# A signed gate maximum in place of absolute gate values, and a new split of gate tiles between two stages

## The reference, cut to what matters

```python
def act_qdq(x):
    qmax = 2.0 ** (ACT_BITS - 1) - 1.0
    scale = jnp.maximum(jnp.max(jnp.abs(x)) / qmax, 1e-12)
    return jnp.clip(jnp.round(x / scale), -qmax - 1.0, qmax) * scale
x = act_qdq(x)
up = act_qdq(x @ lpbq_dequant(w_up).T)
gate = act_qdq(x @ lpbq_dequant(w_gate).T)
sig = fixed_qdq_u16(jax.nn.sigmoid(gate))
gate = act_qdq(gate * sig)
o = act_qdq(gate * up)
return o @ lpbq_dequant(w_down).T
```

## Time and profile before

| | us |
|---|---|
| median of three executions | 1949.89 |
| lowest and highest of them | 1949.58 and 2811.03 |
| the profiled execution, timed from outside | 1950.04 |
| its span, first to last instruction | 1948.1 |
| TensorE busy in the span | 1710.1 (88%) |
| VectorE busy | 1481.2 (76%) |
| ScalarE busy | 1187.5 (61%) |
| GpSimd busy | 809.7 (42%) |

### The profile page before, as it was taken

One profiled execution on the slowest core, in us unless ns is written; L12 is line 12 of the kernel. 1 busy time (PEld: TensorE's weight loads), 2 busy tenths in 40 slices (PEclk: granted clock), 3 DMA queues, 4 the chain that ended last, 5 costly groups with the idle time before them and its releaser, 6 DMA issues. The chain is left out here.

```text
span 1948.1 us, 25419 instructions
## 1 busy us (share of the span) xinstructions
PE 1710.1 (88%) x9112; PEld 659.3 (34%) x9112; DVE 1481.2 (76%) x2113; ACT 1187.5 (61%) x1911; POOL 809.7 (42%) x442
## 2 busy tenths in 40 slices
PE   0899999999999999999968999999999910299999
PEld 0222333323333333333214454544444400044444
DVE  5899888888888888888745665548999998855452
ACT  2376677767777777776642232229997678854441
POOL 3388888978889888886610010100000000000000
PEclk9999999999999999999988999999999965599999
DMA  5477786756776766766344556648785357755542
GB/s 152 92 191 191 164 192 161 160 133 142 183 175 152 164 152 142 169 158 139 69 129 162 185 190 206 183 143 268 254 268 192 120 180 258 237 179 177 168 163 76
DMA packets 188157, 332.17 MB, mean 171 GB/s; under 512 B 27488, under 2 KB 106720, under 8 KB 179520
## 3 DMA queue, kind: packets, MB, share of 16 engines
q1 hardware_dynamic: 179104, 265.54, 44.2%
q0 software_dynamic: 8928, 65.02, 16.7%
HBM read 171.90 MB, written 93.45 MB: 136 GB/s over the span
## 5 line engine op out<-in xcount | busy, mean ns | idle before, releaser
L1070 ACT ACTIVATE P<-quad 128x512 f32<-128x512 f32 x1024 | 557.3, 599 | 222.2 <-PE quad L893 219.4
L1251 DVE TENSOR_REDUCE cm<-quad 128x1 f16<-128x1024 f32 x512 | 600.9, 1216 | 97.9 <-PE quad L881 96.8
L1762 POOL TENSOR_TENSOR Ps<-P,P 128x2048 f32<-128x2048 f32 x93 | 422.8, 4546 | 145.0 <-ACT P L1070 144.8
L893 PE MATMUL quad<-QA,KA 101*128 101x512 f16 x1024 | 352.8, 385 | 7.7 <-ACT P L1070 6.7
L881 PE MATMUL quad<-KA,QA 100*128 100x512 f16 x1024 | 329.0, 392 | 32.1 <-issue 12.9
L1028 PE MATMUL quad<-Wd,oh 128*128 128x512 f16 x768 | 231.7, 382 | 127.8 <-DVE ol L1603 127.6
L929 PE MATMUL quad<-P,cg 128*32 128x512 f32 x2048 | 273.1, 605 | 3.5 <-ACT numT L1098 0.6
L1144 ACT ACTIVATE ev<-quad 128x1024 f32<-128x1024 f32 x96 | 97.5, 1015 | 214.5 <-PE quad L989 209.7
L1486 DVE TENSOR_REDUCE mxt<-ev 128x1 f32<-128x1024 f32 x96 | 116.8, 1217 | 113.3 <-ACT ev L1144 113.2
L989 PE MATMUL quad<-x_hi,Wg 128*128 128x512 f16 x768 | 189.7, 382 | 3.6 <-DVE x_lo L1482 3.6
L893 PEld LDWEIGHTS quad<-QA,KA 101*128 101x128 f16 x1024 | 86.0, 97 | 299.3 <-ACT P L1070 210.3
(11 more groups left out here) (144 smaller groups left out, 2147.1 us busy)
## 6 DMA issues: line engine op xcount, KB each, us to landing
Ps<-P POOLq DMA_DIRECT2D x62, 1024.0 KB, 7.9
gate_scratch<-ev SPq DMA_DIRECT2D x48, 512.0 KB, 2.9
gt<-gate_scratch SPq DMA_DIRECT2D x48, 512.0 KB, 5.5
up_scratch<-ev SPq DMA_DIRECT2D x48, 512.0 KB, 3.0
uf<-up_scratch SPq DMA_DIRECT2D x48, 512.0 KB, 5.0
uf<-up_scratch SPq DMA_DIRECT2D x96, 256.0 KB, 3.6
KA<-part_scratch SPq DMA_DIRECT2D x48, 256.0 KB
QA<-part_scratch SPq DMA_DIRECT2D x48, 256.0 KB
```

What stands on the lines that cost most here:

```text
L893: e.matmul(K.score[h % 2], K.KA[p % 2][0:101, h, 128 * kt:128 * kt + 128], K.QA[p % 2][0:101, qc, h, :], start=True, stop=True).then_inc(K ...
L1070: e.activation(K.Pb[pb][:, h, :], K.score[h % 2], ACT.Exp, scale=SCALE / (QPOW * KPOW)).then_inc(K.a_exp, 1)
L1251: e.tensor_reduce(cm[:, u:u + 1], K.quad[UNIT["max", hm, u] % 2][:, :], AX.X, ALU.max).then_inc(K.v_max, 1)
L1762: e.tensor_tensor(K.Ps[n][:, :, :], K.Pb[(st.g - 1) % NP][:, :, :], K.Pb[st.g % NP][:, :, :], ALU.add).then_inc(K.g_sum, 1)
```

## The change

The largest absolute product of gate and sigmoid is found in another way. The gate times its sigmoid grows with the gate wherever it is positive, so the largest positive product belongs to the largest signed gate value. That value is now found in the gate stage by a second pass over each evicted tile (`highest`), is made one number for all partitions (`s_row`) and put through the same rounding and sigmoid on a single column. The largest negative product is found by the old instruction with a factor of -1, straight from `gq`. So neither engine makes absolute values of the gate. The 48 gate tiles are handled in 25 steps of up, 42 tiles are gated in the other 23, and six (`LATE`) are left over: two ahead of the product loop, four beside its first products. In the product stage the absolute values have four buffers instead of two, and ScalarE makes its ones three tiles ahead, the first three before the scale of up is known.

```diff
@@ -30,7 +30,7 @@
 NXF, NEV, GW = 4, 3, 1024
 NGT, NSG = 3, 2
 NUF, NUQ, NXR = 4, 3, 3
-LATE = 14
+LATE = 6
 
 
 
@@ -276,7 +276,7 @@
 
 
 ALL = 9
-ALL_NO = {n: ALL * (k + 1) for k, n in enumerate(("w0", "x_row", "w1", "w2", "g_row", "h_row", "u_row", "o_row"))}
+ALL_NO = {n: ALL * (k + 1) for k, n in enumerate(("w0", "x_row", "w1", "w2", "g_row", "s_row", "h_row", "u_row", "o_row"))}
 
 
 R1, R2 = 9, 9
@@ -336,13 +336,17 @@
         self.nwt = [A(f"nwt{i}", [128, 8], F32) for i in range(4)]
         self.nwu = [A(f"nwu{i}", [128, 8], F32) for i in range(4)]
         self.ymax = A("ymax", [128, NT], F32)
-        self.red = A("red", [128, 10], F32)
+        self.red = A("red", [128, 12], F32)
         self.spread = A("spread", [128, 32], F32)
         self.turned = A("turned", [32, 128], F32)
         self.qs = A("qs", [128, 24], F32)
         self.wmx = A("wmx", [128, 12], F32)
         self.mxt = A("mxt", [128, 48], F32)
-        self.mxg = A("mxg", [128, 48], F32)
+        self.mxs = A("mxs", [128, 48], F32)
+        self.mxg = A("mxg", [128, 49], F32)
+        self.top = A("top", [128, 1], I16)
+        self.tops = A("tops", [128, 1], F32)
+        self.topq = A("topq", [128, 1], U16)
         start = A.at
 
 
@@ -409,7 +413,6 @@
         self.gt = [A(f"gt{i}", [128, GW], F32) for i in range(NGT)]
         self.sgm = [A(f"sgm{i}", [128, GW], F32) for i in range(NSG)]
         self.sgq = [A(f"sgq{i}", [128, GW], U16) for i in range(NSG)]
-        self.gab = [A(f"gab{i}", [128, GW], I16) for i in range(2)]
         assert A.at <= gq_at
         A.at = gt_at
         self.Wd = [A(f"Wd{i}", [128, OT, H], F16) for i in range(2)]
@@ -425,7 +428,7 @@
         A.at = x2s_at
         self.wl.append(A("wl3", [128, 512], F32))
         self.prt = [self.ol[0][:, 4 * i:4 * i + 4, :].rearrange("p a n -> p (a n)").bitcast(F32) for i in range(2)]
-        self.pab = [self.ol[1][:, 2 * i:2 * i + 2, :].rearrange("p a n -> p (a n)").bitcast(I16) for i in range(2)]
+        self.pab = [self.ol[1][:, 2 * i:2 * i + 2, :].rearrange("p a n -> p (a n)").bitcast(I16) for i in range(4)]
 
         def sem(name):
             return ctx.enter_context(nc.semaphore(name))
@@ -461,7 +464,7 @@
         self.a_num, self.a_den, self.a_wh = sem("a_num"), sem("a_den"), sem("a_wh")
         self.a_wn, self.a_wi = sem("a_wn"), sem("a_wi")
         self.a_xhi, self.a_ev, self.a_gq = sem("a_xhi"), sem("a_ev"), sem("a_gq")
-        self.a_sig, self.a_gab, self.a_uabs = sem("a_sig"), sem("a_gab"), sem("a_uabs")
+        self.a_sig, self.a_top, self.a_uabs = sem("a_sig"), sem("a_top"), sem("a_uabs")
         self.a_pab, self.a_uq, self.a_oh = sem("a_pab"), sem("a_uq"), sem("a_oh")
 
         self.v_aux, self.v_bias, self.v_st1, self.v_mv1 = sem("v_aux"), sem("v_bias"), sem("v_st1"), sem("v_mv1")
@@ -470,7 +473,7 @@
         self.v_sum, self.v_st2, self.v_mv2, self.v_ymax = sem("v_sum"), sem("v_st2"), sem("v_mv2"), sem("v_ymax")
         self.v_wmax, self.v_wsc, self.v_wmul, self.v_wrnd = sem("v_wmax"), sem("v_wsc"), sem("v_wmul"), sem("v_wrnd")
         self.v_wl, self.v_xc, self.v_xq, self.v_xlo = sem("v_wl"), sem("v_xc"), sem("v_xq"), sem("v_xlo")
-        self.v_mx, self.v_sgq, self.v_gab, self.v_gmax = sem("v_mx"), sem("v_sgq"), sem("v_gab"), sem("v_gmax")
+        self.v_mx, self.v_sgq, self.v_top, self.v_gmax = sem("v_mx"), sem("v_sgq"), sem("v_top"), sem("v_gmax")
         self.v_g2, self.v_q, self.v_pab, self.v_pmax = sem("v_g2"), sem("v_q"), sem("v_pab"), sem("v_pmax")
         self.v_oq, self.v_ol, self.v_out, self.v_all = sem("v_oq"), sem("v_ol"), sem("v_out"), sem("v_all")
 
@@ -537,7 +540,7 @@
     ("sx", "rx", "fg", "fu", "gv", "sg", "gr", "rg", "f2", "g2v", "s2", "g2r", "r2",
      "uv", "su", "ur", "ru", "fo", "ov", "so", "orr", "ro", "fin"))}
 Q_OPS = ("x_row", "x_s", "x_r", "fg", "fu",
-         "g_row", "g_v", "g_s", "g_r0", "g_r", "f2",
+         "g_row", "g_v", "g_s", "g_r0", "g_r", "f2", "s_row",
          "h_row", "h_v", "h_s", "h_r0", "h_r",
          "u_row", "u_v", "u_s", "u_r0", "u_r",
          "o_row", "fo", "o_v", "o_s", "o_r0", "o_r", "fin")
@@ -548,7 +551,7 @@
 
     plan, done = [], 0
     for step in range(1, 49):
-        until = 48 * step // 28 if step <= 28 else 48 + (48 - LATE) * (step - 28) // 20
+        until = 48 * step // 25 if step <= 25 else 48 + (48 - LATE) * (step - 25) // 23
         plan.append(range(done, until))
         done = until
     assert done == 96 - LATE
@@ -556,13 +559,12 @@
 
 
 GATE_PLAN = gate_plan()
-GAB_ON_ACT = [n % 12 in (0, 2, 5, 7, 10) for n in range(48)]
 PAB_ON_ACT = [n % 16 * 11 % 16 < 11 for n in range(48)]
 
 
-def gab_no(n):
-
-    return sum(GAB_ON_ACT[i] == GAB_ON_ACT[n] for i in range(n + 1))
+def mx_no(k):
+
+    return 2 * k + 2 if k < 48 else 49 + k
 
 
 def pab_no(n):
@@ -571,7 +573,7 @@
 
 def g2_tail():
 
-    return range(48 - LATE, 52 - LATE), {n: 52 - LATE + n // 2 for n in range(48) if n % 2 == 1 and 52 - LATE + n // 2 < 48}
+    return range(48 - LATE, 50 - LATE), {2 * i + 1: 50 - LATE + i for i in range(LATE - 2)}
 
 
 TODO = [(ch, ot) for ch in range(NCH) for ot in range(OT)]
@@ -1139,7 +1141,7 @@
     def evict(k, nq):
         e.wait_ge(K.pe_prj, k + 1)
         if k >= NEV:
-            e.wait_ge(K.v_mx, k - NEV + 1)
+            e.wait_ge(K.v_mx, mx_no(k - NEV))
             e.wait_ge(K.d_ev[k % NEV], 16 * (k // NEV))
         e.activation(K.ev[k % NEV][:, :], K.quad[k % nq][:, :], ACT.Copy).then_inc(K.a_ev, 1)
 
@@ -1181,15 +1183,27 @@
                     e.activation(view(n), K.gt[n % NGT][:, :], ACT.Copy, scale=rg).then_inc(K.a_gq, 1)
                     e.wait_ge(K.a_gq, n + 1)
                     sigmoid(n, n)
-                    if GAB_ON_ACT[n]:
-                        if n >= 2:
-                            e.wait_ge(K.v_gmax, n - 1)
-                        e.activation(K.gab[n % 2][:, :], view(n), ACT.Abs).then_inc(K.a_gab, 1)
+                    if n == 1:
+
+                        e.wait_ge(K.v_all, ALL_NO["s_row"])
+                        e.activation(K.top[:, :], K.red[:, 11:12], ACT.Copy, scale=rg).then_inc(K.a_top, 1)
+                        e.wait_ge(K.a_top, 1)
+                        e.activation(K.tops[:, :], K.top[:, :], ACT.Sigmoid, scale=sg).then_inc(K.a_top, 1)
                 else:
                     sigmoid(n - 48, n)
+    def gate_abs(n):
+        if PAB_ON_ACT[n]:
+            e.wait_ge(K.v_g2, n + 1)
+            if n >= 4:
+                e.wait_ge(K.v_pmax, n - 3)
+            e.activation(K.pab[n % 4], view(n), ACT.Abs).then_inc(K.a_pab, 1)
+
     first, beside = g2_tail()
     for n in first:
         sigmoid(n, 48 + n)
+    e.wait_ge(K.pe_prj, 96)
+    for n in range(3):
+        gate_abs(n)
     e.wait_ge(K.v_q, Q_NO["u_r"])
     uf_uses = 0
     for n in range(48):
@@ -1200,11 +1214,8 @@
         uf_uses += 1
         if n in beside:
             sigmoid(beside[n], 48 + beside[n])
-        if PAB_ON_ACT[n]:
-            e.wait_ge(K.v_g2, n + 1)
-            if n >= 2:
-                e.wait_ge(K.v_pmax, n - 1)
-            e.activation(K.pab[n % 2], view(n), ACT.Abs).then_inc(K.a_pab, 1)
+        if n + 3 < 48:
+            gate_abs(n + 3)
 
     def quantize_up(n):
         u = 48 + n
@@ -1441,7 +1452,7 @@
 
     def global_max(src, name):
 
-        k = 2 * ("x_row", "g_row", "h_row", "u_row", "o_row").index(name)
+        k = 2 * ("x_row", "g_row", "h_row", "u_row", "o_row", "s_row").index(name)
         e.tensor_reduce(K.red[:, k:k + 1], src, AX.X, ALU.max).then_inc(K.v_q, 1)
         e.wait_ge(K.v_q, Q_NO[name])
         everywhere(K.red[:, k + 1:k + 2], K.red[:, k:k + 1], name)
@@ -1484,6 +1495,10 @@
     def largest(k, col):
         e.wait_ge(K.a_ev, k + 1)
         e.tensor_reduce(K.mxt[:, col:col + 1], K.ev[k % NEV][:, :], AX.X, ALU.max, apply_absolute_value=True).then_inc(K.v_mx, 1)
+
+    def highest(k, col):
+
+        e.tensor_reduce(K.mxs[:, col:col + 1], K.ev[k % NEV][:, :], AX.X, ALU.max).then_inc(K.v_mx, 1)
 
     for n in range(NXF):
         quant_x(n)
@@ -1501,6 +1516,7 @@
                 for n in range(4, 8):
                     low_x(n)
             largest(12 * cp + ot, 4 * ot + cp)
+            highest(12 * cp + ot, 4 * ot + cp)
             if cp < 3:
                 n = 8 * cp + 8 + ot
                 if 1 <= ot < 9:
@@ -1517,11 +1533,12 @@
                     weight_now(job)
     e.wait_ge(K.v_wsc, wsc_no(1, 6))
     e.tensor_tensor(sc["fu"], sc["sx"], K.wmx[:, 6:7], ALU.mult).then_inc(K.v_q, 1)
-    e.wait_ge(K.v_mx, 48)
+    e.wait_ge(K.v_mx, mx_no(47))
     bg = global_max(K.mxt[:, :], "g_row")
     e.wait_ge(K.v_q, Q_NO["fu"])
     quant_scale(bg, sc["fg"], ("gv", "sg", "gr", "rg"), ("g_v", "g_s", "g_r0"))
     e.tensor_scalar(sc["f2"], sc["sg"], 1.0 / 65536.0, None, ALU.mult).then_inc(K.v_q, 1)
+    global_max(K.mxs[:, :], "s_row")
 
     def view(n):
         return K.gq[:, n // 4, GW * (n % 4):GW * (n % 4) + GW]
@@ -1541,44 +1558,47 @@
```

(27 more changed lines are left out.)

## The result

| | us |
|---|---|
| after, median of four executions | 1965.5 (1963.77 to 1965.94) |
| before, median of four executions | 1949.74 |
| ratio after to before | 1.0083, 95% interval 1.0063 to 1.0102 |
| profiled execution, span | 1963.5, before 1948.1: +15.4 |

One of the four executions of the kernel before was a slow one of 2811.03 us, which the ratio leaves out.

The account below looks back on a forecast made before the run. TensorE bounds the gate and down stages, VectorE ends up, ScalarE and VectorE alternate in products. Gate +15.4, up +2.0, products -12 sum to +5.4 on 1949.9: 1955 us, own range 1947 to 1963, widened for rivals to 1942 to 1966.

Parts of the forecast that it names:

- Gate stage, +15.4: Gate stage: 48 added maxima on VectorE delay weight turns by 12.3 us and two tiles of x by 3.1.
- The step that carried it: Gate stage: mean period is the larger of TensorE's own and half the turn-to-eviction-to-ready chain; 12.3 us over 24 steps.
- The rival that the pass hides in idle time: Gate stage: the signed maximum fits VectorE's 1.76 us idle per step, stage adds 1, total 1941; chance 0.14.
- First part of up, -18.0: First up eviction to maximum of gated products: absolute values removed, ScalarE sets the pace, about 146 us; -18.0.
- The 11 us of waits: First part of up: gate loads, taken at 5.8 us each, delay ScalarE by 11 us over 25 steps.
- The 3.2 us for a load of 512 KB: First part of up: skill's load estimate, by which no step would wait; prediction set it aside for the trace's 5.5.
- Second part of up, +18.9: Maximum of gated products to maximum of up: 42 tiles and 22 maxima instead of 34 and 19; +18.9.
- Product stage, -12: Maximum of up to maximum of products: 101.4 us instead of 113.3, bounds -18 and -6.
- Then only ScalarE limits: Product stage after the first 27.85 us: ScalarE's own work of 65.7 us sets the pace, total 95 before load waits.
- The clock rival: Gate stage: TensorE's clock falls in new stalls, 33 us on top if every weight step paid, 1988; chance 0.05.
- That the product maximum costs more with -1: Up stage: product maximum slower with factor -1 than 1, first 0.1 us per tile hidden by ScalarE; chance 0.01.
- The loads as the bound: Transfers bind in up's first part (+9) or the product stage (+5): 1960 to 1970, say 1965; chance 0.14.

Follow-up runs that it names:

- four buffers show it: The kernel after with four instead of three buffers for gate tiles, loaded three tiles ahead; 1957.4 us, ratio 1.0039 to the kernel before.
- the load latency and the split of the tiles mended too: The kernel after with pass last, six absolute-value buffers, four gate-tile buffers, and two left-over tiles instead of six; 1927.17 us, ratio 0.9884.

## Why the prediction was right, and where it was off

- *Gate stage, +15.4.* Measured +15.5. The step that carried it, that a weight block made one step ahead sets the period to half of two chained stretches, is confirmed by two experiments: the pass alone brings the 15.5 into the kernel before, and the same pass behind the weight block gives 13.2 of them back. The evictions came alternately 6.25 and 5.92 us apart in weight steps without x, a mean of 6.08 as worked out, and 7.21 and 6.55 with x, a mean of 6.88. The waits of the turns for GpSimd, which were to be 10 to 15 us, are 9.4, just under.
- *The rival that the pass hides in idle time* is refuted as it stood, and yet the idle time was real. What decided was where in the order the pass stood.
- *First part of up, -18.0.* Measured -17.7. The 11 us of waits held (10.4, at a median load of 5.6 us where 5.8 was taken), and so did the rest of the sum: with 0.4 us of waits the part takes the 135.1 that were worked out. That latency and not bandwidth made these waits was a choice of the prediction between two readings; four buffers show it.
- *The 3.2 us for a load of 512 KB.* The Trainium skill, DMA: Bandwidth & Descriptors, on the anatomy of one DMA, fits its 2.0 us plus bytes over 436 GB/s per DMA and for DMAs issued by GpSimd. These loads are issued by SyncE and share the transfer engines with others; here the median is 5.6 us, and 6.0 with one more load in flight, so the estimate does not fit them. How much of the difference is sharing no run takes apart.
- *Second part of up, +18.9.* Measured +18.8.
- *Product stage, -12.* Measured -1.7, outside its bounds of -18 to -6; at 111.5 us the stage was over the 107 that the prediction named as a sign of being wrong. This is the term that failed. The step is "Then only ScalarE limits", with "the four buffers of absolute values do away with the small mutual waits": the sum took ScalarE's mean per tile (and VectorE's for the first eight) as if each engine could work on while the other is busy. The prediction had the diff's wait before it and did not follow what is queued behind it: with four buffers and a lead of three, up's next value stands behind a gate value that waits for VectorE, and a round of three tiles takes 5.95 us instead of ScalarE's 5.05. First eight tiles: 32.2 us from the maximum of up to the start of the ninth product, forecast 27.9; the 4.2 us more are VectorE's two waits for the sigmoid of a left-over tile, which ScalarE makes behind the same waits. The other forty: 79.3, forecast 73.5, although 6.5 of that were for loads, which cost 3.1. With one more buffer the same two stretches take 27.8 and 70.7, the stage 98.5: within 3 us of the forecast's 101.4.
- *The clock rival* is refuted: behind waits of 0.98 us the next four matmuls take 1.03 us (row at 1236.91), and the granted clock is 1.00 from 1045 to 1326, as it was before; over the span it is 0.960 against 0.958. The Trainium skill, TensorE: Matmul & The Clock Gate, on a second failure mode, has short idle moments between groups of matmuls make the clock swing; with the idle moments of up to 1.43 us in this stage that did not show.
- *That the product maximum costs more with -1* is refuted by the groups of the two kernels, first before, then after (busy us, mean ns of one | idle):

```profile
L1552 DVE CUSTOM_DVE_ANT_0 sgm<-gab,sgq 128x1024 f32<-128x1024 int16 x48 | 58.8, 1225 | 4.0 <-ACT gab L1187 0.4
...
L1565 DVE CUSTOM_DVE_ANT_0 sgm<-gq,sgq 128x1024 f32<-128x1024 int16 x48 | 58.8, 1225 | 1.6
```

- *The loads as the bound* was given 0.14; the time fell where that rival had it (1960 to 1970), but not for its reason: loads cost ScalarE 3.1 us in the product stage, less than before, and their median in the up stage was 5.6 us, not 6.5. That the time still lies in the range is luck: the upper end was moved from 1963 to 1966 for this rival.

So the change did what it should to the amount of work, and lost it in two places of order: 15.5 us in the gate stage, which the prediction had, and 11 to 13 in the product stage, which it had not. With both mended it is 0.6% faster than the kernel before, with the load latency and the split of the tiles mended too it is 1.2%.

## What to carry to other kernels

Idle time on an engine is usable only behind the work for which another engine is waiting: put an added pass last in its step, and before costing it at nothing look up what stands behind it in its queue. When work is made ahead into a ring of buffers, count buffers less lead; that difference is the room one engine has to run ahead of the other. With one tile of room the pace was that of the chain through both engines, 5.95 us for three tiles; with two it was that of the slower engine alone, 5.00. Take a cause away and look at what binds next: VectorE, then TensorE, then VectorE again ended the same stage within three small edits.

## What the runs showed of the hardware

- The same loads of 512 KB landed later on median (6.0 against 5.6 us) with one more in flight, and the stage still got 11.4 us shorter, at 296 GB/s with the transfer engines busy 0.87 of the time. The busy share of 0.83, at 272 GB/s, in the kernel after was no limit.
- The product maximum with the factor -1, reading the int16 gate itself, takes the same 1225 ns in mean over 48 tiles as with 1.
- TensorE's granted clock stayed at 1.00 through the 281 us of the gate stage from 1045 on, with single waits of 0.29 to 1.43 us ahead of its matmuls.
